# Second batch's Sinkhorn steps moved to GpSimd, the first batch's done alone on VectorE

## What is computed

```
x = x + L0_xattn(layernorm(x), ctx)              # quantised product
h = layernorm(x)                                 # four streams of 256 columns
L = rms_norm(h) @ [W_res, W_pre, W_post].T + base    # 24 logits a token
H_res = sinkhorn(L[:16] / 0.1, 50 iterations)    # 4 x 4 per token, rows and columns in turn
H_res = (1 - g) I + g H_res
y = (softmax(L[16:20]) . streams) @ W_branch     # the branch
x = x + H_res . streams + y * softmax(L[20:24])  # mixing, and the branch's share
x = x + attention(layernorm(x), ctx)             # Q K^T as x M ctx^T with M = Wq^T Wk
x = x + ffn(layernorm(x))                        # LoRA, 2752 hidden
```

## Time and profile before

| | before |
|---|---|
| median of three runs | 1237.05 us |
| the profiled execution: time, span | 1240.85 us, 1239.0 us |
| PE busy, share of the span | 1177.8 us, 95% |
| VectorE busy | 797.4 us, 64% |
| ScalarE busy | 479.5 us, 39% |
| GpSimd busy | 128.8 us, 10% |
| mean granted clock of PE | 0.979 |

### The profile page before, as it was taken

How to read it: one execution, slowest core, us unless ns; L and a number is a source line. 1 busy time by engine, 2 the same in 40 slices (tenths; PEclk the granted TensorE clock), 3 DMA queues, 4 the chain that set the end, 5 groups by cost and what they waited for, 6 DMA issues and landing times.

```text
span 1239.0 us, 16460 instructions
## 1 busy us (share of the span) xinstructions
PE 1177.8 (95%) x6394; PEld 584.9 (47%) x6394; DVE 797.4 (64%) x1571; ACT 479.5 (39%) x718; POOL 128.8 (10%) x176
## 2 busy tenths in 40 slices
PE   3989999789999999999999999999999999999998
PEld 2435554464444445455444444444444444444444
DVE  7685898989998246887776767767767652222220
ACT  7773752565135223534434334344343231111110
POOL 4410250018101310020000000000001000000000
PEclk9878999889999999999999999999999999999999
DMA  9530000014003214220111110211210241111310
GB/s 371 209 111 1 2 2 1 1 69 136 35 8 112 64 31 141 69 102 5 65 69 58 46 69 34 69 69 34 69 52 24 63 143 46 47 46 46 117 44 23
DMA packets 26063, 83.58 MB, mean 67 GB/s; under 512 B 3649, under 2 KB 4289, under 8 KB 25985
## 3 DMA queue, kind: packets, MB, share of 16 engines
q1 hardware_dynamic: 25984, 82.53, 19.6%
HBM read 76.22 MB, written 6.29 MB: 67 GB/s over the span
## 4 chain that ended last, share of the span: by engine, by line
PE 72%; DVE 20%; ACT 4%; issue 2%; POOL 1%; DMA 1%; SPq 0%; ACTq 0%; DVEq 0%
PE PAIR L2256 31%; PE PAIR L1896 10%; PE PAIR L1898 10%; PE PAIR L1897 10%; DVE LORA L1294 5%; DVE LORA L1293 4%; DVE LORA L1292 4%; PE PAIR L1961 2%; DVE X L1340 2%; PE PAIR L2213 2%; PE PAIR L1978 1%; PE PAIR L2090 1%; PE PAIR L1969 1%; PE PAIR L2268 1%; PE PAIR L2002 1%
## 5 line engine op out<-in xcount | busy, mean ns | idle before, releaser
L1896 PE MATMUL PAIR<-POOL 128*128 128x512 f16 x688 | 262.4, 381 | 4.3 <-DVE POOL L1383 2.4
L1898 PE MATMUL PAIR<-POOL 128*128 128x512 f16 x688 | 262.0, 381 | 0.0
L1897 PE MATMUL PAIR<-POOL 128*128 128x512 f16 x688 | 261.8, 381 | 0.0
L2256 PE MATMUL PAIR<-XT,POOL 128*128 128x512 f16 (+1 forms) x1056 | 239.0, 379 | 1.0 <-ACT ST L867 1.0
L2256 PEld LDWEIGHTS PAIR<-XT,POOL 128*128 128x128 f16 (+1 forms) x1056 | 102.5, 98 | 120.6 <-issue 2.5
L2256 PE MATMUL PAIR<-X,POOL 128*128 128x512 f16 (+1 forms) x528 | 121.2, 379 | 0.0
L1898 PEld LDWEIGHTS PAIR<-POOL 128*128 128x128 f16 x688 | 67.3, 98 | 82.4 <-issue 1.6
L1896 PEld LDWEIGHTS PAIR<-POOL 128*128 128x128 f16 x688 | 67.2, 98 | 76.1 <-issue 5.5
L1897 PEld LDWEIGHTS PAIR<-POOL 128*128 128x128 f16 x688 | 67.4, 98 | 65.1 <-issue 1.6
L1511 DVE SCALAR_TENSOR_TENSOR STG<-STG,PAIR 128x1024 f32<-128x1024 f32 (+2 forms) x32 | 28.1, 884 | 93.5 <-PE PAIR L2268 89.2
L901 ACT ACTIVATE POOL<-STG 128x1024 f16<-128x1024 f32 (+2 forms) x32 | 25.0, 788 | 146.2 <-DVE STG L1511 146.2
(11 more groups left out here) (281 smaller groups left out, 1733.7 us busy)
## 6 DMA issues: line engine op xcount, KB each, us to landing
STG<-in_gate_w SPq DMA_DIRECT2D x21, 512.0 KB, 3.6
STG<-in_up_w SPq DMA_DIRECT2D x21, 512.0 KB, 4.3
STG<-in_ctx_t SPq DMA_DIRECT2D x16, 512.0 KB, 3.6
STG<-in_ctx SPq DMA_DIRECT2D x16, 512.0 KB, 3.7
STG<-in_down_w SPq DMA_DIRECT2D x16, 512.0 KB, 3.5
POOL<-in_ctx SPq DMA_DIRECT2D x12, 512.0 KB, 10.9
X<-in_x SPq DMA_DIRECT2D x8, 512.0 KB, 9.6
out_t<-X SPq DMA_DIRECT2D x16, 256.0 KB, 2.9
```

Source lines behind the costliest of these rows:

```text
L1896: e.matmul(dst, l_hi, r_hi, start=first, stop=False)
L1897: e.matmul(dst, l_hi, r_lo, start=False, stop=False)
L1898: return e.matmul(dst, l_lo, r_hi, start=False, stop=last)
L2256: i = e.matmul(dst, blk[:, a_, k, :], src[:, b_, k, :], start=(opens and k == 0 and n == 0), stop=(k == KD // 2 - 1 and n == 2), skip_grou ...
```

## The change

GpSimd now makes all 99 steps of the second batch, in place of VectorE. It has five instructions a step: two adds that sum four entries, a power of -1, a scaling, and a multiply, each waiting for the one before. It makes four steps before each `branch_sum` from tile 2 on, goes on to step `PAUSE` = 56, waits until the first batch is mixed (`mixed` at 4), and makes the rest. VectorE makes the first batch's 99 steps on 64 columns, and writes the reciprocals to `PAIR[2]`. For that M's blocks use pairs 0 and 1 only, and other tiles change pairs too. `add_share` becomes a DMA on GpSimd's queue that accumulates in SBUF, each waiting for the one before. All context differences are VectorE's. The second batch's logits are made in two pairs of tiles, with the last pair behind the row sums, and its last two transposes within M's first block. `mix_diag(2)` stands before `mix_help(1)`, the diagonals of tile 3 lie elsewhere (`DGM`), and `m_rest(7)` stands between the mixing products. `maximum(0)` stands behind the mixing of tile 4. The diff, without its lines on names of semaphores and of the identity's signals:

```diff
@@ -214,10 +214,10 @@
-        DGM = [v[:, 0:(NST - 1) * NST * P].rearrange("p (j i t) -> p j i t", j=NST - 1, i=NST) for v in (
-            T4B[:, :, :, :].rearrange("p s k t -> p (s k t)").bitcast(F32),
-            STG[:, 0:2, :].rearrange("p n d -> p (n d)"))]
-        MIX_PAIR = (None, None, 0, 2)
+        DGM = [v.rearrange("p k t -> p (k t)").bitcast(F32)[:, 0:(NST - 1) * NST * P]
+               .rearrange("p (j i t) -> p j i t", j=NST - 1, i=NST) for v in (
+                   T4B.rearrange("p s k t -> p (s k) t"), XT[:, 0, 1, :, :])]
+        MIX_PAIR = (None, None, 2, 1)
@@ -227,6 +227,8 @@
+        NTOK = BT * NST
+        MINUS = SM[:, 320:320 + NTOK]
@@ -240,6 +242,10 @@
+        def part(b):
+            return ZP[:, b * NE:(b + 1) * NE]
@@ -330,8 +336,8 @@
-        M_PAIR = (2, 1, 0, 2, 1, 0, 2, 1)
-        T3_PAIR = (1, 3, 0, 2)
+        M_PAIR = (1, 0, 1, 0, 1, 0, 1, 0)
+        T3_PAIR = (3, 0, 2, 1)
@@ -507,30 +514,49 @@
-                    e.wait_ge(lg_p, 1 + BT)
+                    e.wait_ge(lg_p, 3)
...
-                e.tensor_tensor(b_[:, CST:half], b_[:, CST:half], b_[:, half + CST:D], ALU.add).then_inc(p_step, 1)
-                e.wait_ge(p_step, 6 + g)
+                step(e.tensor_tensor(b_[:, CST:half], b_[:, CST:half], b_[:, half + CST:D], ALU.add))
...
+            ticks = [5]
+            def step(i):
+                i.then_inc(p_step, 1)
+                ticks[0] += 1
+                e.wait_ge(p_step, ticks[0])
+            def sinkhorn_step(n):
+                z, half, sums, rec = part(1), ZE[:, 0:2 * NTOK], ZE[:, 2 * NTOK:3 * NTOK], ZE[:, 3 * NTOK:4 * NTOK]
+                if n % 2:
+                    z3 = z.rearrange("p (r j) -> p r j", j=NST)
+                    h3 = half.rearrange("p (r j) -> p r j", j=2)
+                    step(e.tensor_tensor(h3, z3[:, :, 0:2], z3[:, :, 2:4], ALU.add))
+                    step(e.tensor_tensor(sums, h3[:, :, 0], h3[:, :, 1], ALU.add))
+                    over = rec.unsqueeze(2).to_broadcast([P, NTOK, NST])
+                else:
+                    z3 = z.rearrange("p (i c) -> p i c", i=NST)
+                    step(e.tensor_tensor(half, z[:, 0:2 * NTOK], z[:, 2 * NTOK:4 * NTOK], ALU.add))
+                    step(e.tensor_tensor(sums, half[:, 0:NTOK], half[:, NTOK:2 * NTOK], ALU.add))
+                    over = rec.unsqueeze(1).to_broadcast([P, NST, NTOK])
+                step(e.tensor_tensor(rec, sums, MINUS, ALU.pow))
+                step(e.tensor_scalar(rec, rec, SINK_SCALE, 0.0, ALU.mult, ALU.add))
+                last = e.tensor_tensor(z3, z3, over, ALU.mult)
+                if n < STEPS - 1:
+                    step(last)
+                else:
+                    last.then_inc(sink_p, 1)
...
-                for q in range(0, D, CST):
-                    last = e.tensor_tensor(X[:, g, q:q + CST], X[:, g, q:q + CST], SHARE[g][:, q:q + CST], ALU.add)
-                last.then_inc(share_ok, 1)
-            def context_lo(i):
-                n, kind, b, k = context_item(i)
-                tile = (CN if kind else CTT)[b][k]
-                if i == 2 * KP:
-                    e.wait_ge(c_lo, i)
-                e.wait_ge(c_hi, i + 1)
-                for q in range(0, D, CST):
-                    last = e.tensor_tensor(tile[:, 1, q:q + CST], STAGE[n % SLOTS][:, q:q + CST], tile[:, 0, q:q + CST],
-                                           ALU.subtract)
-                last.then_inc(c_lo, 1)
+                if g:
+                    e.wait_ge(summed, 16 * g)
+                e.dma_start(X[:, g, :], SHARE[g], accum_op=ALU.add).then_inc(summed, 16)
@@ -567,19 +593,24 @@
             centre_q(15)
-            for g in range(NT):
+            branch_sum(0)
+            branch_sum(1)
+            e.wait_ge(sink_v, 4)
+            done = 0
+            for g in range(2, NT):
+                for n in range(done, done + 4):
+                    sinkhorn_step(n)
+                done += 4
                 branch_sum(g)
-                if 4 <= g:
-                    add_share(g - 4)
-            for g in range(BT, NT):
-                add_share(g)
-                if g >= BT + 2:
-                    context_lo(2 * (g - BT - 2))
-                    context_lo(2 * (g - BT - 2) + 1)
-            for i in range(4, KP + 2):
-                context_lo(i)
-            for i in range(2 * KP, 2 * KP + 6):
-                context_lo(i)
+                if g >= BT:
+                    add_share(g - BT)
+            for n in range(done, PAUSE):
+                sinkhorn_step(n)
+            e.wait_ge(mixed, BT)
+            for n in range(PAUSE, STEPS):
+                if n >= STEPS - 4 * BT and (n - STEPS) % 4 == 0:
+                    add_share(NT + (n - STEPS) // 4)
+                sinkhorn_step(n)
             for n in range(N_F, N_F + 8):
@@ -652,10 +683,10 @@
-            def tile_across(t):
-                ts = slice(t * P, (t + 1) * P)
-                e.wait_ge(lg_p, t + 2)
+            def pair_across(t):
+                ts = slice(t * P, (t + 2) * P)
+                e.wait_ge(lg_p, 2 + t // 2)
                 e.wait_ge(lt_p, 1)
@@ -723,9 +754,9 @@
-                    e.wait_ge(lg_p, 1 + BT)
+                    e.wait_ge(lg_p, 3)
...
-                    e.wait_ge(share_ok, 1)
+                    e.wait_ge(summed, 16)
@@ -747,7 +778,7 @@
-                    e.wait_ge(mixed, 1)
+                    e.wait_ge(summed, 16 * BT)
@@ -764,9 +795,9 @@
                 if g == 0:
-                    e.wait_ge(share_ok, BT)
+                    e.wait_ge(summed, 16 * BT)
                 elif g == BT:
-                    e.wait_ge(share_ok, NT)
+                    e.wait_ge(summed, 16 * NT)
                 e.wait_ge(x3t_p, g + 1)
@@ -980,15 +1011,13 @@
-            tile_across(0)
...
+            pair_across(0)
...
-            tile_across(1)
...
-            tile_across(2)
...
-            tile_across(3)
+            pair_across(2)
@@ -1013,9 +1042,9 @@
+                    mix_diag(2)
+                elif n == 14:
...
-                elif n == 14:
-                    mix_diag(2)
@@ -1282,35 +1311,33 @@
-                chain(e.scalar_tensor_tensor(ZP, ZE, SINK_SCALE, ZE, ALU.mult, ALU.mult))
-            def sinkhorn_step(n, z, rs, rr):
+                for b in range(B):
+                    z = ZE.rearrange("p (i b c) -> p i b c", i=NST, b=B)[:, :, b, :]
+                    i = e.scalar_tensor_tensor(part(b).rearrange("p (i c) -> p i c", i=NST), z, SINK_SCALE, z, ALU.mult,
+                                               ALU.mult)
+                    if b:
+                        i.then_inc(sink_v, 1)
+                        e.wait_ge(sink_v, 4)
+            def sinkhorn_step(n):
+                z, sums, rec = part(0), RS[:, 0:NTOK], PAIR[2][:, 0:NTOK]
...
-                    red, over, flat = by_row, over_row, by_row
+                    z3 = z.rearrange("p (r j) -> p r j", j=NST)
+                    red, over = z3, rec.unsqueeze(2).to_broadcast([P, NTOK, NST])
...
-                    red, over, flat = by_column, over_column, flat_column
-                chain(e.tensor_reduce(rs, red(z), AX.X, ALU.add))
-                chain(e.reciprocal(rr, rs))
-                chain(e.scalar_tensor_tensor(flat(z), over(rr), SINK_SCALE, flat(z), ALU.mult, ALU.mult))
-            def part(b):
-                return ZE[:, b * NE:(b + 1) * NE], RS[:, b * n32 // B:(b + 1) * n32 // B], RR[:, b * n32 // B:(b + 1) * n32 // B]
-            def take_apart():
-                for b in range(B):
-                    i = e.tensor_copy(ZE[:, b * NE:(b + 1) * NE].rearrange("p (i c) -> p i c", i=NST),
-                                      ZP.rearrange("p (i b c) -> p i b c", i=NST, b=B)[:, :, b, :])
-                chain(i)
-            def second_steps(n0, n1):
-                for n in range(JOINT + n0, JOINT + n1):
-                    sinkhorn_step(n, *part(1))
+                    z3 = z.rearrange("p (i c) -> p i c", i=NST)
+                    red, over = z.rearrange("p (i c) -> p c i", i=NST), rec.unsqueeze(1).to_broadcast([P, NST, NTOK])
+                chain(e.tensor_reduce(sums, red, AX.X, ALU.add))
+                chain(e.reciprocal(rec, sums))
+                chain(e.scalar_tensor_tensor(z3, over, SINK_SCALE, z3, ALU.mult, ALU.mult))
...
+                if b:
+                    e.wait_ge(sink_p, 1)
...
-                e.scalar_tensor_tensor(HR[:, bs], part(b)[0], col(GSC), OMGI[:, bs], ALU.mult, ALU.add).then_inc(hr_ok, 1)
+                e.scalar_tensor_tensor(HR[:, bs], part(b), col(GSC), OMGI[:, bs], ALU.mult, ALU.add).then_inc(hr_ok, 1)
@@ -1333,7 +1360,7 @@
-                    e.wait_ge(share_ok, g + 1)
+                    e.wait_ge(summed, 16 * (g + 1))
@@ -1377,8 +1404,6 @@
-                if i in (KP + 2, 2 * KP + 6):
-                    e.wait_ge(c_lo, i)
@@ -1644,8 +1669,8 @@
+            add_product(7)
...
-            add_product(7)
@@ -1653,11 +1678,8 @@
             row_terms()
```

(92 more changed lines are left out.)

## The result

| | before | after |
|---|---|---|
| median | 1237.24 us (1236.87 to 1241.43) | 1505.77 us (1504.98 to 1505.97, 4 runs) |
| ratio | | 1.217, 95% interval 1.215 to 1.219 |
| span of the profiled execution | 1239.0 us | 1503.1 us |
| VectorE's factors of the first batch | 231.6 | 214.3 |
| GpSimd's last step | (none) | 594.1 |

The account below looks back on a forecast made before the run. PE holds 72% of the chain, so the prediction sought its waits, chiefly behind VectorE's Sinkhorn steps. Gains of 10.6 and 3.0 us, 13.6 in sum, took 1237.05 to 1223.5 us; range 1218 to 1240.

Parts of the forecast that it names:

- pow taken as an add: GpSimd's second-batch steps: five instructions priced from memset and add rows, 0.90 us plus 0.40 for waits, 1.3 a step.
- upper bound of 4.05: GpSimd's step at most 4.05 us: five instructions of 0.81 us each; the lower bound was 0.55.
- Rival A: GpSimd's step is long, above all pow; VectorE waits before the second batch's factors; 1268 at 2.0 us; chance 0.19 slower.
- When GpSimd is due: Second batch's steps: GpSimd done at 309.5, due by 318.6, 9 us to spare; late from 1.51 us a step.
- Branch tiles: M's half rounds: lag of four steps, a sum and an issue, 8.4 us against 6.6, stays within 13 us.
- First batch: VectorE's 99 steps at 0.82 us, reciprocals in PSUM not hit by GpSimd: 134.3 to 215.5, not 231.6.
- Rival B: First batch's PSUM reciprocals: 10 us more over 99 steps, 1228, chance 0.08; or multiplies stretched by GpSimd, 10 slower, 0.02.
- To project(0): Mixing: PE's 8.4 us wait before the mixing product goes, project(0) starts at 262.1 instead of 272.71; gain 10.6 us.
- logits in pairs: Second batch's logits: no gain from pairing itself; PE loses a 0.45 us wait and M ends 0.45 earlier.
- rival C: Two transposes before project(0) and the stretch behind at full clock: 3 to 4 us more gain, 1220; chance 0.12.
- Projection, share: Projection: PE's waits behind the steps go, 3.0 us; shares by DMA land in 3.7 us, hidden.
- The sum: Whole kernel: 10.6 + 3.0 = 13.6 us gained, from 1237.05 to 1223.5.

Follow-up runs that it names:

- e1: Changed kernel with each GpSimd pow replaced by a multiply of constants and the scaling by 1 (second batch's factors wrong): 1240.36 us.
- e10: Changed kernel with GpSimd's pow and scaling replaced by one tensor_scalar, a first-order reciprocal (second batch's factors approximate): 1220.88 us.
- e5: e1 with VectorE's maximum(0) ahead of the second batch's factors instead of behind mix(4): 1235.50 us.
- e12: e10 with maximum(0) ahead of the second batch's factors, the order of e5: 1218.26 us.
- e6: e1 without the scaling, so four GpSimd instructions a step: 1222.27 us.
- e7: Changed kernel with real pow, GpSimd making 14 second-batch steps, VectorE the other 85, context differences back on GpSimd: 1248.36 us.
- e4: e1 with shares added by GpSimd's four adds a tile instead of DMAs: 1254.08 us.
- e8: e7 with 18 second-batch steps on GpSimd and 81 on VectorE: 1245.20 us.
- e9: e8 with GpSimd's ten context differences ahead of the DMAs that add shares 4 to 7: 1229.44 us.
- e11: e8 in its order, but GpSimd waits for the share DMA to land before the run of adds: 1237.29 us.

## Why the prediction was wrong

**The step that failed** is "pow taken as an add" in *GpSimd*. The term is five instructions, 0.90 us, and 0.40 for waits. The pow in it was 0.15 us and is 2.93; the other four were 0.75 and are 1.00; the waits were right. So 4.3 us stand against 1.3, beyond even the upper bound of 4.05, which took every instruction as dear as an add of 256 columns. That bound was the real fault: the nearest rows were of other operations, and width is no measure of what an operation costs. 16 columns of pow cost four times what 256 of an add do. Rival A named the instruction, the place and the sum (at p = 4.3 its end is 139.6 + 17.2 + 8 + 99 x 4.3 = 590.5; measured 594.1), but was given 0.19.

**When GpSimd is due.** 318.6 was forecast; e1 shows 310.7, e10 307.9. In either profile 2.3 to 2.4 us of that are no error: the execution was so much ahead before its first reordered instruction (below). The rest has two parts: M starts some 3 us earlier than the forecast had it, and the forecast counted the due time back from the second batch's norm, while the wait that decides is at `maximum(0)`, put behind mix(4) by the same change. e5 shows the second part, 4.9 us; e12 agrees in kind. So lateness does not begin at 1.51 us a step but between 1.30 (e6, no wait) and 1.38 (e10, 3.0 us).

**Branch tiles.** The lag of four steps, a sum and an issue against M's half rounds was said to stay within 13 us. At 1.3 or 1.6 us a step it does (e1 and e6 have no such wait); at 4.3 PE lost 54.7 us there. No rival had this second place.

**First batch.** Right: 0.829 for 0.82 us a step, no stretching, the factors at 214.3 for 215.5. The start at 132.25 shows that the logits did not come 2 us later as worked out: they do against M's start (8.8 us behind it, not 5.8), but M itself starts 3.0 us earlier. Rival B's bounds fall: PSUM costs 8 ns a write and none at the read.

**To project(0).** Right in kind: no wait of PE before the mixing product (e1, e6), where the earlier trace rows had 8.4 us. ScalarE reaches the factors at 217.0 in e1, not 221.2. Over e1, e6 and e10 project(0) starts 15.9 to 18.7 us earlier, not 10.6, but that is three things. PE's transposes of tile 5 and its first product of M, before and in e1:

```profile
102.52 1.04 PE L1978 MATMUL PAIR<-IDF,X 128*128 128x128 f32 x8
...
126.45 0.38 PE L1896 MATMUL PAIR<-POOL 128*128 128x512 f16 x1
```
```profile
100.26 1.04 PE L2000 MATMUL PAIR<-IDF,X 128*128 128x128 f32 x8
...
121.25 0.39 PE L1918 MATMUL PAIR<-POOL 128*128 128x512 f16 x1
```

Up to the first row PE's order is the same in both, and the profile after has 102.49 there: that 2.3 us (4.2 in e6, 2.4 in e10) is the difference of executions. From there to M took 23.9 us before and 21.0 in e1, e6, e10 and the profile after. So the logits in pairs go with some 3 us, where 0.45 had been forecast; how much of it is the order and how much the clock (mean 0.86 over the stretch before, 0.92 after) stays open with one profile of before. And from M to project(0) it took 146.3 us before and 135.6 to 135.7 in e1 and e6: 10.6 us, the forecast. The term was right. Of rival C, the two slow transposes come at full clock in e10 (3.84 us, and 13.3 us gained from M on) and not in e6 or e12 (6.55 and 6.58).

**Projection, share.** The 3.0 us wait is gone. A share lands 4.6 us after its issue, where 3.7 had been the nearest row, and the issue holds GpSimd for 0.92 to 1.07 us (0.85 to 1.18 in e7), where 1 had been guessed. Hidden, as forecast; e4 shows 13.7 us of worth while GpSimd is late.

**The sum** nearly holds with its own premise: 13.6 us of gain were forecast, and e6 measured 14.4 (interval 12.5 to 16.2). That it is so near is in part luck: with the 3 us at M's start the parts add up to some 16.6, and e10 and e12, with about the same step, measured 16.6 and 18.4. Where e6 loses 2 us of it isn't shown.

## What to carry to other kernels

An operation that no trace shows has no nearest row: bound it from above by what another kind of operation could cost, or measure it alone before it goes 99 times in a chain. Where work moves to an idle engine, work out from what duration of a step on it is late, at every place that waits for it, and look which consumer's order puts something else behind that wait. And keep GpSimd's own DMAs away from runs of GpSimd adds when VectorE works on two SBUF inputs.

## What the runs showed of the hardware

- GpSimd's pow on 128 partitions: 1.02 us for 4 columns, 2.93 for 16. Its other small instructions in the same steps: 0.20 to 0.32 us for 16 to 64 columns, and 0.08 more for a wait on the one before.
- A VectorE multiply with two SBUF inputs was held to the end of a run of 24 GpSimd instructions (15.19 us) when the run followed straight on a DMA issued by GpSimd (e7, e8), and lasted about as long as one of them (0.6 to 0.7 us) otherwise (e9, e11). The Trainium skill (SBUF — State Buffer, "SBUF: two separate sides") says that the one who comes second waits for the whole of the other's instruction. The 0.65 us agree; the 15.19 us, over 24 instructions, go beyond it.
- VectorE's reductions and reciprocals, with one input, ran on beside such GpSimd runs at 0.22 to 0.26 us (e9's run of 24); the reciprocal ahead of the held multiply in e7 took 0.25.
